# A 64-column inverse transform table in place of one padded with zeros, in a spectral vision kernel

## What is computed

```python
x_ft = jnp.fft.rfft2(x, norm='ortho')
out = jnp.einsum('bixy,ioxy->boxy', x_ft[:, :, :M1, :M2], w)      # M1 = M2 = 20
out_ft = jnp.zeros((B, w.shape[1], H, W // 2 + 1)).at[:, :, :M1, :M2].set(out)
x1 = jnp.fft.irfft2(out_ft, s=(H, W), norm='ortho')
x2 = jnp.einsum('bchw,oc->bohw', x, cw) + cb[None, :, None, None]
x = gelu(x1 + x2)
```

## Time and profile before

| | us |
|---|---|
| median of 3 runs | 1156.59 (1151.57 to 1160.94) |
| span of the profiled execution | 1153.2 |
| TensorE matmul busy | 1066.4 |
| TensorE load busy | 710.0 |
| VectorE busy | 615.4 |
| ScalarE busy | 409.8 |
| GpSimd busy | 137.3 |

### The profile page before, as it was taken

The page is one execution under the profiler, slowest core; times in us unless marked ns, Lnnn a source line. Parts: engine busy times, 40 slices in busy tenths (PEclk is TensorE's granted clock), DMA queues, the critical chain, the costliest instruction groups (busy, mean ns, idle before and its releaser), DMA issues.

```text
span 1153.2 us, 34262 instructions
## 1 busy us (share of the span) xinstructions
PE 1066.4 (92%) x15860; PEld 710.0 (62%) x15860; DVE 615.4 (53%) x773; ACT 409.8 (36%) x554; POOL 137.3 (12%) x127
## 2 busy tenths in 40 slices
PE   5899999999999999999899999989999899689996
PEld 4578767767776733577668767867524788632221
DVE  2238445833854322358337635833234467768887
ACT  2332223123222377232232223223485777421100
POOL 6000000000000000000000000020000564334421
PEclk9999999999999999999999999999999899869999
DMA  5220030022002400310220031020001000000000
GB/s 183 88 73 3 17 122 25 2 87 73 3 13 91 132 4 13 111 45 3 83 78 2 2 112 49 3 74 30 1 16 50 1 2 2 2 1 1 1 10 10
DMA packets 25652, 46.62 MB, mean 40 GB/s; under 512 B 9437, under 2 KB 10488, under 8 KB 24869
## 3 DMA queue, kind: packets, MB, share of 16 engines
q1 hardware_dynamic: 24694, 43.49, 12.2%
q10 hardware_dynamic: 384, 0.66, 0.2%
q0 software_dynamic: 432, 0.29, 0.1%
HBM read 30.25 MB, written 10.89 MB: 36 GB/s over the span
## 4 chain that ended last, share of the span: by engine, by line
PE 76%; DVE 11%; ACT 4%; issue 3%; DMA 2%; POOL 2%; SPq 2%; ACTq 0%; POOLq 0%; DVEq 0%
PE PSALL L1250 22%; PE PSALL L1109 9%; PE PSALL L1218 7%; PE PSALL L1126 7%; DVE WORK L1442 5%; PE PSALL L1328 4%; PE PSALL L1241 4%; PE PSALL L498 4%; PE PSALL L1194 4%; PE PSALL L401 3%; PE PSALL L1338 2%; DMA WORK<-MIXED 2%; PE PSALL L486 2%; DVE WORK L1461 2%; PE PSALL L380 2%
## 5 line engine op out<-in xcount | busy, mean ns | idle before, releaser
L1461 DVE STREAM_TRANSPOSE WORK<-PSALL 128x1024 f32<-128x1024 f32 x128 | 152.4, 1229 | 318.1 <-PE PSALL L1218 318.1
L1250 PEld LDWEIGHTS PSALL<-EW,WORK 64*128 64x128 f32 x4096 | 250.0, 193 | 65.5 <-issue 48.3
L1250 PE MATMUL PSALL<-EW,WORK 64*128 64x128 f32 x4096 | 266.1, 283 | 12.8 <-DVE WORK L1461 12.8
L1378 ACT ACTIVATE X<-PSALL,TABLES 128x1024 f32<-128x1024 f32 x128 | 141.7, 1114 | 331.9 <-PE PSALL L1250 331.9
L1442 DVE STREAM_TRANSPOSE WORK<-PSALL 128x1024 f32<-128x1024 f32 x100 | 119.1, 1229 | 58.3 <-PE PSALL L1109 54.5
L1126 PE MATMUL PSALL<-TABLES,WORK 128*128 128x128 f32 x1000 | 138.4, 287 | 4.9 <-DVE WORK L1442 0.5
L1126 PEld LDWEIGHTS PSALL<-TABLES,WORK 128*128 128x128 f32 x1000 | 120.7, 194 | 32.1 <-issue 18.3
L1359 ACT COPY SPEC<-PSALL 128x400 f32<-128x400 f32 x64 | 53.5, 846 | 175.6 <-PE PSALL L1126 172.4
L1109 PE MATMUL PSALL<-WORK,DW 32*64 32x256 f32 x3200 | 103.3, 389 | 12.4 <-DMA B<-in_fc_b 12.4
L1438 DVE STREAM_TRANSPOSE WORK<-X 128x1024 f32<-128x1024 f32 x96 | 111.3, 1203 | 0.0
L678 POOL MEMSET SW<- 64x4160 f32 x1 | 3.6, 3559 | 748.3 <-PE PSALL L1202 748.3
(11 more groups left out here) (148 smaller groups left out, 969.0 us busy)
## 6 DMA issues: line engine op xcount, KB each, us to landing
SW<-in_spec_w SPq DMA_DIRECT2D x160, 80.0 KB, 2.4
spec_scr<-MIXED SPq DMA_DIRECT2D x24, 400.0 KB, 3.2
SPEC<-spec_scr SPq DMA_DIRECT2D x32, 200.0 KB
WORK<-spec_scr SPq DMA_DIRECT2D x16, 200.0 KB
WORK<-MIXED SPq DMA_DIRECT2D x64, 40.0 KB
WORK<-in_coords_w SPq DMA_DIRECT2D x2, 1024.0 KB, 5.0
XC<-in_coords_c SPq DMA_DIRECT2D x2, 1024.0 KB, 7.4
hid_scr<-WORK SPq DMA_DIRECT2D x64, 8.0 KB
```

What stands on the lines that cost most here:

```text
L1250: m = pe.matmul(PS[2 * p + z][:, 2 * b * GRID:(2 * b + 2) * GRID], G[64 * z:64 * z + 64, n % 2, b, h:h + 4, :, c].rearrange("p q o -> p (q ...
L1378: nc.scalar.activation(X[:, n].rearrange("p b (z d) c w -> p d z b (c w)", z=2)[:, p, :, :, 2 * t * GRID:2 * (t + 1) * GRID], PSALL[:, 2 * ...
L1461: nc.vector.transpose(G[:, n % 2, 2 * x + y].rearrange("p h o v -> p o h v"), PSALL[:, 4 + 2 * x:6 + 2 * x, :].rearrange("p k (h o v) -> p ...
```

## The change

The table loses its two blocks of zeros: it has 64 columns, is loaded as such, and every call streams all of it. Each call now writes only the 64 PSUM columns of its own pixel row: row parity c of image b stands at columns (2 b + c) x 64. Stationary operands, the number and order of calls, semaphores and buffers stay; the instruction lists of VectorE, ScalarE and GpSimd are the same, and SyncE's differs in the one transfer of the table.

```diff
-        EW = sb("EW", [128, 3 * GRID])
+        EW = sb("EW", [128, GRID])
...
                 for c in range(2):
                     h = 4 * (2 * p + t)
                     for z in range(2):
-                        m = pe.matmul(PS[2 * p + z][:, 2 * b * GRID:(2 * b + 2) * GRID],
+                        m = pe.matmul(PS[2 * p + z][:, (2 * b + c) * GRID:(2 * b + c + 1) * GRID],
                                       G[64 * z:64 * z + 64, n % 2, b, h:h + 4, :, c].rearrange("p q o -> p (q o)"),
-                                      EW[64 * z:64 * z + 64, (1 - c) * GRID:(3 - c) * GRID],
+                                      EW[64 * z:64 * z + 64, :],
                                       start=False, stop=True, skip_group_check=True, tile_position=(64 * z, 0))
...
-        "idft_w": np.pad(idft_w.reshape(128, GRID), ((0, 0), (GRID, GRID))).astype(f), "ident": np.eye(128, dtype=f),
+        "idft_w": idft_w.reshape(128, GRID).astype(f), "ident": np.eye(128, dtype=f),
```

## The result

The changed kernel is slower: 1168.2 us (median; 1166.6 to 1172.2) against 1156.3 us, a ratio of 1.0105 with a 95% interval of 1.008 to 1.013.

> The changed kernel once more, beside the other two on the same chip: 1166 to 1170 us, ratio 1.009 to 1.013; if the dips of its first profile were an accident of those executions, 1153 us.

The account below looks back on a forecast made before the run. TensorE was taken to bound the kernel, through L1250's bursts. Span 1153.2 - 4.0 = 1149.2 us, plus 3.4 us from span to median, gave 1152.6 us; own range 1147 to 1161, 8-in-10 range 1136 to 1161.

Parts of the forecast that it names:

- The step: In bursts of L1250, the time from one load to the next stays 118 ns, set by the load of 128 stationary columns.
- The rival in which the stream sets the step: In L1250's bursts, time per load and matmul halves with the columns to 59 ns: 1031.6 us; chance 0.08.
- the one in which the halves slide apart: In L1250's bursts, each row half loads without waiting for the other: 111 ns each, 14.3 us less, 1138.3 us; chance 0.08.
- the first rival: In L1250's bursts, the stream sets the pace: 59 ns in place of 118, 121 us less, 1031.6 us; chance 0.08.
- The burst ends: At 72 ends of L1250 bursts, the last stream ends 0.055 us sooner: 4.0 us saved, bounds 0 to 4.2.
- one sign to look for: L1250's matmul records should have a median near 220 to 225 ns in place of 278, still 4096 of them.
- The clock: Emptier bursts might lower TensorE's granted clock; the forecast counted nothing, the rival 24 us, 1176.6 us, with chance 0.06.
- the third rival: Emptier bursts of L1250 lower the granted clock, one dip of six us per layer run: 24 us more, 1176.6 us; chance 0.06.
- The median: For the whole kernel, the 3.4 us between profiled span and median of the runs was carried over, giving 1152.6 us.

## Why the prediction was wrong

- **The step.** Right. Load and stream were told apart by the first record of a burst (105 ns on an idle array) and by the step of 118 against L1126's 111. The runs show it directly: the step is the same with 128, 64 and 32 columns streamed, and 60 ns with 64 stationary columns. The rival in which the stream sets the step is out, and so is the one in which the halves slide apart: the step did not come down to 111. One reading was wrong on the way. The trace of before does have a line with a load much longer than its stream, the transposes of the tail, and its step is short: four loads of L320 (65 * 128 stationary, 65 x 65 moving) start at 985.42 us and last 0.33 us, the last of them 0.145, which makes (0.33 - 0.145) / 3 = 62 ns. This would have spoken for the first rival. It did not hold for L1250, whose loads last 193 ns. Why the step is 118 and not 111 was not tried; the account given for it, loads that begin when both halves' matmuls have begun, stays unproved.
- **The burst ends.** Right: 0.37 us for the seven later sets of a layer run without a dip, 0.053 each against 0.055. Over all 56 it was 2.5 us, since some dips reached into a later set. But one sign to look for was wrong. The matmul record did not fall to 220 ns; its median stayed at 278, with half the columns. Only the first record of a burst became shorter, 328 ns for 382. So the length of a record in the middle of a burst is not its stream's.
- **The clock.** This is the step that failed: the sum put the clock at nothing. The rival was named, with the emptier bursts but not the wait beside them, and was given a chance of 0.06. Its price, 3 us for a dip of 6, was near: three dips of 10.2 us cost 3.0 to 3.3 us each and two of 3.4 us 1.0 and 1.1. The argument against it compared an average round of the later sets (65% streamed) with the forward half (72%). A fuller stretch that keeps its clock does not vouch for an emptier one; but the later sets did keep 1.00, so the conclusion was right for the place that it spoke of. It never looked at the first set. There the trace of before already had TensorE idle for 1.36 us ahead of the first burst, and the narrow bursts beside that wait are where the clock fell and the time went: 11.7 us in one trace, 17.3 in the other. The price of an edit that empties the array belongs to the emptiest place in which it acts, not to the mean one. The prediction's own sign of being wrong, a step under 110 ns, did not come; the sign of the third rival, a clock under 1.00 between 50 and 800 us, did.
- **The median.** The 3.4 us between the profiled span and the median came again (1168.2 - 1164.7 = 3.5), but by luck. A run's time stands only 1.8 to 2.0 us above its own span; the rest is that the profiled execution was quicker than the median, in the changed kernel the quickest of four.

## What to carry to other kernels

Columns of zeros streamed beside a load that takes as long cost next to nothing here, and taking them away saved nothing but the last stream of each burst; first ask whether the load or the stream sets the step, by halving one of them. And where a matmul-bound kernel has bursts next to waits, work that looks wasted may be what keeps the clock. What did best here was both: take it out only where TensorE runs without a pause, and put filler into the wait.

## What the runs showed that was not expected

A full busy share did not mean a full clock: with 32 columns streamed PE was busy 40.00 of 40 us, and the granted clock was 0.71. And the response is steep. Beside loads of 128 columns, streams of 128 kept 1.00 in the layers of the profile of before; streams of 64 lost it in the first sets and at the heads, and kept it in all later sets; streams of 32 lost it in later sets as well, and that one run took 170 us more than the kernel before. The loads of a burst kept the same step all the while.
